# One attention stage of a six-stage kernel: order of the TensorE work in a slot, and order of the heads

## The reference, cut to what matters

```python
def proj(w):                      # 16 heads, D_K = 8, S = 1024, B = 2
    return jnp.einsum('bsd,ed->bse', x, w).reshape(B, S, NUM_HEADS, D_K).transpose(0, 2, 1, 3)
Q, K, V = (proj(w_q), proj(w_k), proj(w_v))
scores = jnp.einsum('bhqd,bhkd->bhqk', Q, K) / jnp.sqrt(jnp.float32(D_K))
attn = jax.nn.softmax(scores, axis=-1)
out = jnp.einsum('bhqk,bhkd->bhqd', attn, V)
out = out.transpose(0, 2, 1, 3).reshape(B, S, D)
out = jnp.einsum('bsd,ed->bse', out, w_o) + b_o
return _layer_norm(x + out, ln_g, ln_b)
```

## Time and profile before

| | us |
|---|---|
| median of 3 runs (4200.23 to 4219.9) | 4217.46 |
| profiled execution, its own time | 4211.42 |
| its span | 4209.6 |
| TensorE matmul busy | 3890.5 (92%) |
| attention stage, first query scores to last transpose | about 3590 to 4110 |

### The profile page before, as it was taken

One profiled execution on the slowest core, in us unless ns is written; L12 is line 12 of the kernel. 1 busy time (PEld: TensorE's weight loads), 2 busy tenths in 40 slices (PEclk: granted clock), 3 DMA queues, 4 the chain that ended last, 5 costly groups with the idle time before them and its releaser, 6 DMA issues.

```text
span 4209.6 us, 151591 instructions
## 1 busy us (share of the span) xinstructions
PE 3890.5 (92%) x65521; PEld 2422.8 (58%) x65521; DVE 3375.9 (80%) x6704; ACT 2736.0 (65%) x4940; POOL 2091.0 (50%) x1202
## 2 busy tenths in 40 slices
PE   6999999999999999589999999999999987899985
PEld 3666666666666666456666666666666654333333
DVE  7988888888888888588888888888888875577745
ACT  4767767777677676157777676776777752366662
POOL 4656656566666565066566565665656630000000
PEclk9999999999999999799999999999999997599997
DMA  4112121121121211111121211212111110000000
GB/s 101 40 34 55 40 55 37 38 58 36 40 55 40 55 35 39 27 28 40 34 59 41 55 35 40 55 40 54 37 38 37 36 32 1 0 1 1 1 1 10
DMA packets 131142, 153.71 MB, mean 37 GB/s; under 512 B 67480, under 2 KB 90408, under 8 KB 128816
## 3 DMA queue, kind: packets, MB, share of 16 engines
q1 hardware_dynamic: 130480, 144.02, 15.0%
HBM read 35.93 MB, written 1.05 MB: 9 GB/s over the span
## 4 chain that ended last, share of the span: by engine, by line
PE 63%; DVE 24%; issue 7%; ACT 4%; POOL 0%; DVEq 0%; SPq 0%; POOLq 0%; DMA 0%; ACTq 0%
PE psum L377 10%; DVE turn L658 9%; PE psum L446 8%; PE psum L388 8%; PE psum L413 6%; DVE den L716 5%; PE psum L438 4%; DVE nmax L694 4%; PE psum L366 4%; PE psum L1274 3%; PE psum L509 3%; PE psum L1262 3%; PE psum L516 3%; PE psum L526 3%; PE psum L1264 2%
## 5 line engine op out<-in xcount | busy, mean ns | idle before, releaser
L658 DVE TENSOR_TENSOR turn<-psum,ropes 128x512 f32<-128x512 f32 x1536 | 938.5, 673 | 6.2 <-POOL qkr L783 4.2
L790 POOL TENSOR_TENSOR turn<-turn 128x1024 f32<-128x1024 f32 x384 | 903.2, 2373 | 25.7 <-DVE turn L658 25.7
L545 ACT ACTIVATE sq<-psum 128x512 f32<-128x512 f32 x768 | 456.1, 594 | 541.8 <-PE psum L366 541.8
L802 POOL TENSOR_TENSOR scratch<-scratch,rden 128x1024 f32<-128x1024 f32 x192 | 365.3, 1903 | 883.0 <-DVE rden L719 883.0
L366 PE MATMUL psum<-wqkv,xT 128*128 128x512 f32 x1536 | 767.7, 623 | 31.8 <-DVE turn L658 30.2
L783 POOL TENSOR_TENSOR qkr<-turn,rn 128x1024 f32<-128x1024 f32 x384 | 728.1, 1917 | 19.6 <-DVE rn L679 19.4
L388 PEld LDWEIGHTS psum<-ident,qkr 128*128 128x128 f32 x3072 | 335.1, 143 | 347.1 <-issue 166.0
L377 PE MATMUL psum<-wqkv,xT 128*64 128x512 f32 x1536 | 433.8, 644 | 65.3 <-DVE turn L658 53.5
L388 PE MATMUL psum<-ident,qkr 128*128 128x128 f32 x3072 | 473.6, 288 | 7.6 <-POOL qkr L783 6.8
L684 DVE TENSOR_REDUCE ss<-sq 128x16 f32<-128x1024 f32 x384 | 448.9, 1211 | 0.0
L425 PEld LDWEIGHTS psum<-scratch,Vs 64*64 64x64 f32 (+1 forms) x12288 | 327.0, 134 | 183.0 <-issue 180.6
(11 more groups left out here) (191 smaller groups left out, 6420.1 us busy)
## 6 DMA issues: line engine op xcount, KB each, us to landing
Vs<-V SPq DMA_DIRECT2D x384, 128.0 KB
Vs<-V SPq DMA_DIRECT2D x768, 64.0 KB
wqkv<-in_L_ffn_Wqkv_dram SPq DMA_DIRECT2D x12, 1536.0 KB
wo<-in_L_ffn_Wo_dram SPq DMA_DIRECT2D x48, 128.0 KB
zs<-Y SPq DMA_DIRECT2D x192, 31.8 KB
w<-in_L_ffn_W_dram SPq DMA_DIRECT2D x12, 341.0 KB
zs<-Y SPq DMA_DIRECT2D x168, 0.2 KB
w<-in_L_ffn_W_dram SPq DMA_DIRECT2D x12, 128.0 KB
```

The source lines that it names most:

```text
L545: act.activation(sq[:, q // 2, q % 2, :, :], bank[QK_BANK[q]][:, :].rearrange("p (h d) -> p h d", d=RH), ACT.Square).then_inc(sem("squared ...
L658: e = dve.tensor_tensor(dst, src, tab.unsqueeze(1).broadcast_to([P, HEADS, RH]), ALU.mult)
L790: pool.tensor_tensor(t1, t1, turn2[:, w, :, :, :].rearrange("p a h d -> p (a h d)"), ALU.add).then_inc(sem("added"), 1)
```

## The change

In odd slots the order on TensorE becomes: `turn_max` (where there is one), scores of the first key tile, `weigh`, less-max of the first key tile, the slot's query unit, scores and less-max of the second key tile. In slots without `weigh` the query unit still precedes the key tiles, but `turn_max` and `turn_out` now precede the query unit. The head of query unit u is UNIT_ROWS[u % 4] with (2, 0, 3, 1) in place of u % 4, on TensorE and in the column where DVE puts the maximum. The orders of ACT and DVE are not edited.

```diff
--- before.py
+++ after.py
@@ -1136,6 +1136,7 @@
         GROUPS, SECTIONS = BATCH * H2 // GQ, 2 * BATCH * H2 // GQ
         LEAD, KEPT = 20, 12
         S2_BANK, RING, O_BANK = (0, 2), (4, 5, 6), 7
+        UNIT_ROWS = (2, 0, 3, 1)
         SLOTS2 = range(-LEAD - 4, 16 * SECTIONS + 5)
 
         at_yT = flat(kT[:, :, :, :])
@@ -1233,16 +1234,17 @@
                           at_yT[:, SEQ * b + 512 * h:SEQ * b + 512 * h + 512], start=True, stop=True).then_inc(
                     sem("at_proj"), 1)
 
-            def scores2(u):
-                n, t, r = u // 32, u // 4 % 8, u % 4
-                if u % 32 == 0:
-                    pe.wait_ge(sem("at_stacked"), 2 * n + 2)
-                if u >= 2:
-                    pe.wait_ge(sem("at_maxed"), u - 1)
-                for h in range(2):
-                    mm = pe.matmul(bank[S2_BANK[u % 2] + h][:, :], qst[n % 2][32 * r:32 * r + 32, P * t:P * t + P],
-                                   kst[n % 2][32 * r:32 * r + 32, 512 * h:512 * h + 512], start=True, stop=True)
-                mm.then_inc(sem("at_scores"), 1)
+            def scores2(u, h):
+                n, t, r = u // 32, u // 4 % 8, UNIT_ROWS[u % 4]
+                if h == 0:
+                    if u % 32 == 0:
+                        pe.wait_ge(sem("at_stacked"), 2 * n + 2)
+                    if u >= 2:
+                        pe.wait_ge(sem("at_maxed"), u - 1)
+                mm = pe.matmul(bank[S2_BANK[u % 2] + h][:, :], qst[n % 2][32 * r:32 * r + 32, P * t:P * t + P],
+                               kst[n % 2][32 * r:32 * r + 32, 512 * h:512 * h + 512], start=True, stop=True)
+                if h:
+                    mm.then_inc(sem("at_scores"), 1)
 
             def turn_max(i):
                 r = RING_OF["max", i]
@@ -1261,6 +1263,10 @@
                     pe.wait_ge(sem("at_m"), i + 1)
                 pe.matmul(bank[b][:, :], kst[n % 2][32 * r:32 * r + 32, P * kb:P * kb + P],
                           qst[n % 2][32 * r:32 * r + 32, 512 * qh:512 * qh + 512], start=True, stop=False)
+
+            def less_max(v):
+                i, r = v // 32, v % 4
+                b = RING_OF["st", v]
                 pe.matmul(bank[b][:, :], onesr[32 * r:32 * r + 32, :], mrow[i % 2][32 * r:32 * r + 32, :],
                           start=False, stop=True).then_inc(sem("at_st"), 1)
 
@@ -1287,19 +1293,26 @@
             for j in SLOTS2:
                 if proj_fill(j):
                     project(*proj_fill(j))
-                if max_unit(j) is not None:
-                    scores2(max_unit(j))
+                u, tiles = max_unit(j), exp_tiles(j)
                 if max_section(j) is not None:
                     turn_max(max_section(j))
                 if out_section(j) is not None:
                     turn_out(out_section(j))
-                tiles = exp_tiles(j)
-                for v in tiles[0:1]:
-                    scores_by_key(v)
+                if u is not None and weighed(j) is None:
+                    scores2(u, 0)
+                    scores2(u, 1)
+                if tiles:
+                    scores_by_key(tiles[0])
                 if weighed(j) is not None:
                     weigh(weighed(j))
-                for v in tiles[1:2]:
-                    scores_by_key(v)
+                if tiles:
+                    less_max(tiles[0])
+                if u is not None and weighed(j) is not None:
+                    scores2(u, 0)
+                    scores2(u, 1)
+                if tiles:
+                    scores_by_key(tiles[1])
+                    less_max(tiles[1])
             pe.wait_ge(sem("at_o"), SECTIONS)
             for i in range(4):
                 for j in range(4):
@@ -1393,7 +1406,7 @@
                     (round_high, stack)[k // 2](n, k % 2)
                 u = max_unit(j)
                 if u is not None:
-                    i, c, b = u // 16, P * (u // 4 % 4) + 32 * (u % 4), S2_BANK[u % 2]
+                    i, c, b = u // 16, P * (u // 4 % 4) + 32 * UNIT_ROWS[u % 4], S2_BANK[u % 2]
                     dve.wait_ge(sem("at_scores"), u + 1)
                     if u % 16 == 0 and i >= 2:
                         dve.wait_ge(sem("at_m_turned"), i - 1)
```

## The result

The changed kernel takes 4315.16 us (median of 6, 4299.23 to 4333.66) against 4217.49 before (6 runs): ratio 1.0238, 95% interval 1.0217 to 1.0259. The prediction was 4224, range 4202 to 4243. The granted clock over a whole execution was 0.920 to 0.931 in the six of the changed kernel, and 0.956 in the profiled one of the kernel before. The profiled execution took 4315.83 (span 4314.0), 104.4 us of span more than before. The page's slices show where: the second line is the granted clock in tenths, and the third is that line in the kernel before.

A forecast was written before the change was run, and what follows sets the result against it. It took a loop of waits through key-tile scores, exponentials and the V product, 3.05 us per regular interval, as the bound. Its terms summed to +12.5 us on the profiled 4211.4, giving 4223.9, predicted as 4224, range 4202 to 4243.

The forecast's parts named there:

- rival 4: TensorE idles about 2.4 us at slots 4 and 5 and the clock falls: 4238 to 4250 us, chance 0.13.
- third sign of being wrong: The forecast is wrong if the granted clock changes at other places than before.
- Regular intervals, nothing: V product to V product in regular slots: plus 0.25 minus 0.23, so unchanged at 3.05 us, 74 intervals.
- Transposes of outputs, +1.0 and +1.7: Key-tile scores wait longer for DVE's multiply: +1.0 us in 7 intervals, +1.7 in 6 where DVE also stacks.
- Transposes of the maxima, +0.48: Slot 13's transpose waits for slot 11's query unit, now behind the V product: +0.48 us each, 8 times.
- Projections, -1.53: Slots 27 to 29: head conflict, lone query unit and less-max ahead of V go, -1.53 us per group, 6 times.
- Small terms: ACT's copy of the outputs behind two exponentials, +1.0 us over 14 times; the half-clock stretch, -0.8 us.
- Rival 3: Denser order makes the clock rise earlier, at the stage's first V products: -13 us, alone 4211; chance 0.13.
- The sum: All terms together: +12.5 us on the profiled execution's 4211.4, giving 4223.9; predicted 4224, +0.30%.

The follow-up runs named there:

- experiment 1: Changed kernel with DVE's reciprocal and multiply on the transposed outputs moved ahead of stack and maximum; 4184.18 us, ratio 0.9948 to the kernel before.
- experiment 6: Changed kernel with the query unit ahead of everything again in slots 3 and 4 of each 16; 4262.66 us, ratio 1.0110 to the kernel before.
- experiment 3: Kernel before with the new head order alone; 4225.23 us, ratio 1.0043 to the kernel before, leaving out one execution at 4310.64.
- experiment 10: Kernel before with new heads and DVE's operations on the transposed outputs first; 438.9 us from first to last V product.
- experiment 4: Changed kernel with the old head order 0, 1, 2, 3, so new order alone; 4346.29 us, ratio 1.0343 to the kernel before.
- experiment 9: Changed kernel with old heads and DVE's operations on the transposed outputs first; 453.8 us from first to last V product.
- experiment 12: Kernel before, old order and old heads, with DVE's operations on the transposed outputs first; 444.7 us from first to last V product.
- experiment 2: Kernel before with one more DVE reduction ahead of the maximum in slots with an outputs' transpose and a query unit; 4315.66 us, ratio 1.0276.
- experiment 5: Changed kernel with DVE's operations on the transposed outputs placed between stack and maximum; 4243.95 us, ratio 1.0072 to the kernel before.
- experiment 8: Changed kernel with DVE's outputs operations first and both transposes issued right behind the V product; 4181.00 us, ratio 0.9918 to the kernel before.
- experiment 11: Changed kernel with DVE's operations on the transposed outputs first, measured once more; 440.6 us from first to last V product.

## Why the prediction was wrong, point by point

**The step that failed** is the one that carries the sum over to the total: that work at full clock stays at full clock. It stood in rival 4 ("the clock falls"), with the right place and the right idle time (2.4 us) but a chance of 0.13 and a price of 14 to 26 us, that of one fall. All 12 transposes reached at full clock were followed by a fall, and half clock cost 103.4 us: a single fall was cheaper than my price (8.6 us), but there were 12. I had compared the new idle time with the one gap of 5 us; the better comparison was with the kernel before. There the weight loads at these scores waited 0.4 and 0.76 us, but the matmuls stood idle only 0.32 with a stack, and without one the timeline shows no idle time before them:

```profile
3824.17 0.49 PE L1262 MATMUL psum<-qst,kst 32*128 32x512 f32 x1 [0.32 <-DVE ropes L1412]
```

And I gave the +1.0 us of the slots without a stack no part in it; their 1.39 us of idle time had the same effect. My third sign of being wrong, a granted clock that changes at other places, is the one that came.

**Regular intervals, nothing:** right. One of them, timeline after:

```profile
3718.56 0.50 PE L1270 MATMUL psum<-mrow,onesr 32*128 32x512 f32 x1
3718.56 0.50 PE L1244 MATMUL psum<-kst,qst 32*128 32x512 f32 x1
3718.57 0.49 PE L1264 MATMUL psum<-qst,kst 32*128 32x512 f32 x1
3718.90 0.39 PE L1244 MATMUL psum<-kst,qst 32*128 32x512 f32 x1
...
3719.10 1.08 ACT L1359 ACTIVATE turn<-psum 128x512 f32<-128x512 f32 x2 [1.23 <-PE psum L1270]
...
3719.33 2.36 DVE L1413 TENSOR_REDUCE gel<-psum 128x1 f32<-128x1024 f32 x2 [1.74 <-PE psum L1244]
...
3720.24 0.50 PE L1264 MATMUL psum<-qst,kst 32*128 32x512 f32 x1
...
3720.66 0.62 PE L1280 MATMUL psum<-turn,scratch 128*9 128x512 f32 x4
```

Less-max, query unit and second key tile start side by side; the exponential comes at t0 + 0.54 (forecast 0.53), the next scores at 1.68 (1.67), the interval is 3.07. The second key tile (3718.57) isn't held behind the query unit's second half, which starts at 3718.90 and is issued ahead of it. The Trainium skill, page "TensorE: Matmul & The Clock Gate", section "The mechanism", says that matmuls start in program order; by that it would be held. The measured starts decide, here as in the prediction.

**Transposes of outputs, +1.0 and +1.7:** right in size (5.18 against 4.22, 6.21 against 4.56), and the cause is shown by experiments 1 and 6. **Transposes of the maxima, +0.48:** 4.10 against 3.63, so the size is right, though the terms given for it (0.66 less 0.23) make 0.43. **Projections, -1.53:** 4.93 and 5.38 against 5.16 and 6.77, -1.62. The transpose now follows the projection directly:

```profile
3748.71 1.12 PE L1233 MATMUL psum<-kT,qT 128*128 128x512 f32 x2
...
3749.67 0.60 PE L1254 MATMUL psum<-ident,gel 128*128 128x128 f32 x4
...
3750.20 0.50 PE L1264 MATMUL psum<-qst,kst 32*128 32x512 f32 x1
```

**Small terms:** half-clock intervals took 4.51, as forecast. The copy of the outputs cost 0.18 in its interval, not 0.07 (3.23). With 0.02 in each regular interval, and slot 19's stall, which I had counted at half clock, this is most of the way from +13.3 to +17.0. **Rival 3**, the earlier rise, came true as well, and was buried under the falls: the second V interval is already 3.07, where before the first ten ran at half clock. Its reason, the denser order, isn't what the runs show: the new heads alone, in the old order, bring the early rise (experiments 3 and 10), and the new order with the old heads (3643 and 3640 us, experiments 4 and 9) is no earlier than the old order with them in experiment 12 (3641).

**The sum:** +12.5 was added to the profiled execution and the result named as the median, though that execution lies 6.0 below the median of the runs. Against the median, 4224 is +0.16% and not +0.30%; beside 100 us this is nothing.

## What to carry to other kernels

When an edit makes TensorE wait where it didn't, price the wait at both clocks: here some 24 us of new waiting cost 103 us of half clock. Look for every engine whose in-order queue now holds the released work behind something that the edit made late; moving two short DVE operations ahead of a maximum cured it, and helped the old kernel too. Before judging an order, test it with its stalls removed: the order that lost 98 us then lost 11 with the old heads, and next to nothing within the stage with the new ones.

## What the hardware showed

In stretches where TensorE is busy 95%, this followed idle times of its matmuls at full clock (the profiled execution of each kernel, slots 3 to 243):

```
idle time, us   where                                        fall followed
2.40            after, 6 slots with a stack                  6 of 6
1.90            experiment 4, with a stack                   6 of 6
1.45            experiment 2, with a stack                   6 of 6
1.39            after, without a stack, at full clock        5 of 5
1.34            experiment 4, without a stack                8 of 8
1.27 to 1.28    experiment 5                                 4 of 6
1.10 to 1.12    experiment 2, without a stack                5 of 8
0.98            experiment 6                                 5 of 6
0.93 to 0.96    slot 7 of after and experiments 1, 5, 8, 11  0 of 5
0.90            experiment 3                                 2 of 6
0.83            experiment 8                                 0 of 6
0.32            before, with a stack                         0 of 6
```

So from 1.34 us up every idle time had a fall with it, at 0.83 and below none of these had, and between them the same idle time did both. Two kinds of fall stand outside this: the dip of experiment 3 behind no idle time above 0.20, and one at slot 243, in the last part of the stage without query units, in the changed kernel and in experiment 6, behind 0.45 us that did nothing there in experiment 1. After a fall the clock stayed at half for 3.4 to 75 us, 1 to 14 intervals, in orders that hold full clock once they have it. What decides between a fall and none at the same idle time, these runs don't settle.
